# GRU steps 64 to 495 as loops on TensorE, with their side products in fp16 into one cleared PSUM bank

## The chip, the core and the metric

The kernel runs on one core of a Trainium2 chip, as one program. The metric is the device time in microseconds (us). TensorE has two instruction rows in the profile: PE (matmul) and PEld (weight load, beside the matmuls). DVE is VectorE, ACT is ScalarE, POOL is GpSimd, SP issues transfers.

## The reference, cut to what matters

The whole network is a top-k mask, attention, a GRU and a sampling layer, each added to x. The change touches the last two. x has four batches of 512 steps with 512 features.

```python
def cell(h, x):                       # 512 steps, one after the other
    gi = x @ W_ih + b_ih              # needs no h: "gates in"
    gh = h @ W_hh + b_hh
    i_r, i_z, i_n = jnp.split(gi, 3, axis=-1)
    h_r, h_z, h_n = jnp.split(gh, 3, axis=-1)
    r = jax.nn.sigmoid(i_r + h_r)
    z = jax.nn.sigmoid(i_z + h_z)
    n = jnp.tanh(i_n + r * h_n)
    h_new = (1.0 - z) * n + z * h
    return (h_new, h_new)
...
x = x + GRU(x)                        # this sum is x3 below
ix = (grid + 1.0) * 0.5 * (L - 1)     # then linear sampling along the features:
out = x + w0 * x[..., i0] + w1 * x[..., i1]
```

## The kernel before

The first third of the span (to 760 us) is mask and attention. Then come 512 GRU steps. Features lie on the 128 partitions, in four chunks; h is held as two halves A and B (two chunks each), each split into a high and a low fp16 part, so that the product with W_hh is made in fp16. One step on PE is 96 matmuls of 128 weights columns by 40 moving columns (L1924), in twelve units of eight named by GRU_UNITS: the half of h that is read, the half that is written, and the gate r, z or n. The units that read A come first (32 matmuls), then BA (24, which end the sums of half A), and the last unit is BBn.

What then happens to a half, taking B: the last matmul of BBn lets DVE sum h_n and r (a scan, L1477, `nlineB`); ACT makes the tanh (L930) and puts the next step's gates in into PSUM (L820, `putB`); DVE makes the new h (L1488) and its parts (L1499, `lowB`), which PE reads in the next step. ACT's program is in order: sigmoid A, give A, tanh A, sigmoid B, put A, give B, tanh B, put B, and then whatever else is due in that step.

Beside the recurrence stand side products, one chunk of a contraction per step behind PE's 96 matmuls: "gates" (x times W_ih for a coming stretch of 64 steps, L1832), "rows" and "late" (x3 times the sampling matrix, the output, L1859 and L1872), each an fp32 matmul of 256 moving columns. Four steps make a group. `side_plan` lists them: step 64 to 495 are full of them but for the steps 112 to 127, which have none. Steps 0 to 15 have three of 128 columns each. Groups alternate between two PSUM banks (`SIDE_BANK[number % 2]`); the first product of a group waits until the group two before it was taken (`side_taken`). ACT takes a group (L830 for gates, L841 for rows) behind its put B in the step in which its last product stands. The sampling matrix is made by ACT and POOL in steps 64 to about 106 (L861, L550). DVE adds the finished states to x (L1402).

The whole of PE's program is written out, instruction by instruction. DVE's is too, with alignments (L1453) in it.

## Time and profile before

| | us |
|---|---|
| median of three runs | 2282.22 |
| lowest and highest | 2280.85, 2285.1 |
| the profiled execution, its own time | 2288.73 |
| its span in the trace | 2286.8 |

The page says for every engine its busy time, then a chain of work followed back from the last instruction, then groups of instructions by line. PE has 95% of the span as busy time, the chain is PE at 81%, and more than half of the span is line L1924, the recurrence. A timeline lists instructions in order of time; "x8" means eight in a row, and the second column is from the start of the first to the end of the last. A bracket says how long the engine was idle before, and what ended that.

### The profile page before, as it was taken

What the parts mean: (1) busy time and instruction counts of PE and PEld (TensorE: products, weight loads), DVE (VectorE), ACT (ScalarE), POOL (GpSimd) and SP (SyncE); (2) the same over time, 40 slices, a digit from 0 to 9 for tenths busy, and PEclk for the clock granted to TensorE, in tenths of its full rate; (3) what the DMA queues carried; (4) which work ended last, traced back from release to release, by engine and by line L of the source; (5) the groups of instructions that cost most, each with busy time, mean ns of one, the idle gap of its engine ahead of it and who ended that gap; (6) DMA issues with size and microseconds to landing.
All of it is one profiled execution on the core that took longest, in us unless ns stands there. A gap on an engine that the chain in (4) does not pass through costs nothing.

```text
span 2286.8 us, 130730 instructions
## 1 busy us (share of the span) xinstructions
PE 2172.7 (95%) x56269; PEld 1831.7 (80%) x56269; DVE 1563.6 (68%) x6093; ACT 1207.0 (53%) x5574; POOL 504.3 (22%) x2271
## 2 busy tenths in 40 slices
PE   5768999999989999999999999999999999999998
PEld 3654655545545999999999999999999999999997
DVE  7987968869687466666666666666666667666665
ACT  6765947759467344566444444444444444444443
POOL 2002121021211122233222222222222222222222
PEclk8569999999999999999999999999999999999999
DMA  5000000010010000000000000000000000000000
GB/s 204 3 2 1 1 1 1 1 56 1 1 56 1 22 5 5 5 5 5 5 5 9 5 9 10 5 9 5 9 10 5 10 5 9 10 5 14 12 10 15
DMA packets 8715, 31.51 MB, mean 14 GB/s; under 512 B 1028, under 2 KB 1352, under 8 KB 7880
## 3 DMA queue, kind: packets, MB, share of 16 engines
q1 hardware_dynamic: 7712, 23.07, 2.7%
q8 instruction: 443, 7.26, 1.3%
q14 instruction: 136, 1.11, 0.2%
q10 hardware_dynamic: 424, 0.07, 0.0%
HBM read 18.94 MB, written 4.19 MB: 10 GB/s over the span
## 4 chain that ended last, share of the span: by engine, by line
PE 81%; DVE 12%; ACT 4%; issue 2%; DMA 1%; POOL 0%; SPq 0%; DVEq 0%; POOLq 0%; ACTq 0%
PE psum L1924 53%; PE psum L1832 9%; PE psum L1735 3%; PE psum L1656 3%; PE psum L1698 2%; PE psum L1753 2%; PE psum L1859 2%; PE psum L1719 2%; DVE region_cols L1087 2%; DVE region_cols L1103 2%; DVE top L1280 2%; ACT region_rows L751 1%; PE psum L1675 1%; DMA region_cols<-in_L_cond_W_emb_dram 1%; PE psum L1872 1%
## 5 line engine op out<-in xcount | busy, mean ns | idle before, releaser
L1924 PE MATMUL psum<-partsA,region_w_hh 128*128 128x40 f16 x24576 | 858.2, 179 | 7.2 <-issue 1.7
L1924 PE MATMUL psum<-partsB,region_w_hh 128*128 128x40 f16 x24576 | 858.2, 179 | 2.4 <-issue 1.9
L1924 PEld LDWEIGHTS psum<-partsA,region_w_hh 128*128 128x128 f16 x24576 | 761.7, 96 | 82.2 <-DVE partsA L1499 11.3
L1924 PEld LDWEIGHTS psum<-partsB,region_w_hh 128*128 128x128 f16 x24576 | 726.7, 95 | 5.4 <-issue 3.8
L564 POOL TENSOR_TENSOR region_w_b<-region_w_b 128x16 f32<-128x16 f32 x1022 | 242.6, 237 | 1135.5 <-DVE region_w_b L1488 1135.5
L1462 DVE TENSOR_REDUCE psum<-psum 128x8 f32<-128x32 f32 x1024 | 201.2, 197 | 292.5 <-PE psum L1924 291.3
L916 ACT ACTIVATE mixA<-psum 128x8 f32<-128x8 f32 x512 | 94.7, 185 | 549.7 <-DVE psum L1462 549.7
L930 ACT ACTIVATE region_w_b<-psum 128x8 f32<-128x8 f32 x1024 | 189.3, 185 | 151.2 <-DVE psum L1477 94.1
L1832 PE MATMUL psum<-region_cols,region_w_a 128*128 128x256 f32 (+1 forms) x864 | 252.7, 390 | 1.0 <-DVE region_cols L1269 0.9
L1488 DVE TENSOR_TENSOR_SCAN region_w_b<-giveB,region_w_b 128x40 f32<-128x40 f32 x512 | 123.6, 241 | 128.5 <-ACT region_w_b L930 128.5
L566 POOL COPY region_work<-region_w_b 128x8 f32<-128x8 f32 x1024 | 203.5, 199 | 2.2 <-DVE region_w_b L1488 2.2
L1469 DVE TENSOR_REDUCE psum<-psum 128x8 f32<-128x32 f32 x1024 | 191.1, 187 | 2.2 <-PE psum L1924 0.9
L751 ACT ACTIVATE region_rows<-psum,neg_top 128x512 f32<-128x512 f32 x256 | 173.9, 686 | 28.9 <-POOL neg_top L516 17.5
L1488 DVE TENSOR_TENSOR_SCAN region_w_b<-giveA,region_w_b 128x40 f32<-128x40 f32 x512 | 123.6, 241 | 75.1 <-ACT region_w_b L930 10.1
L1656 PE MATMUL psum<-region_w_a,region_work 128*128 128x512 f32 x384 | 173.7, 605 | 0.0
L1280 DVE TENSOR_REDUCE top<-psum 128x2 f32<-128x1024 f32 x128 | 156.1, 1221 | 22.9 <-PE psum L1719 22.7
L923 ACT ACTIVATE giveB<-psum 128x8 f32<-128x8 f32 x512 | 94.3, 184 | 102.1 <-DVE psum L1469 101.0
L1735 PEld LDWEIGHTS psum<-ident,region_rows 128*128 128x128 f32 x1024 | 119.0, 142 | 35.8 <-issue 19.0
L1477 DVE TENSOR_TENSOR_SCAN psum<-mixA,psum 128x32 f32<-128x32 f32 x512 | 117.0, 228 | 37.2 <-PE psum L1924 1.7
L1735 PE MATMUL psum<-ident,region_rows 128*128 128x128 f32 x1024 | 137.3, 276 | 5.1 <-ACT region_work L796 3.9
L1656 PEld LDWEIGHTS psum<-region_w_a,region_work 128*128 128x128 f32 x384 | 72.2, 193 | 82.7 <-issue 81.8
L1832 PEld LDWEIGHTS psum<-region_cols,region_w_a 128*128 128x128 f32 x864 | 123.4, 189 | 2.3 <-issue 2.1
(234 smaller groups left out, 2590.3 us busy)
## 6 DMA issues: line engine op xcount, KB each, us to landing
region_rows<-in_x_dram SPq DMA_DIRECT2D x4, 1024.0 KB, 11.1
region_w_a<-in_L_cond_W_qkv_dram SPq DMA_DIRECT2D x1, 3072.0 KB, 22.9
region_w_hh<-in_L_cond_W_hh_dram SPq DMA_DIRECT2D x4, 768.0 KB, 6.5
region_w_a<-in_L_cond_W_ih_dram SPq DMA_DIRECT2D x1, 3072.0 KB, 10.2
out_dram<-region_w_b SPq DMA_DIRECT2D x12, 256.0 KB, 3.1
region_cond<-in_cond_dram SPq DMA_DIRECT2D x2, 1024.0 KB, 7.9
region_cols<-in_L_cond_W_emb_dram SPq DMA_DIRECT2D x1, 2048.0 KB, 19.4
region_w_out<-in_L_cond_W_out_dram SPq DMA_DIRECT2D x1, 1024.0 KB, 21.5
```

Of the source, the lines that this page charges most:

```text
L564: e.tensor_tensor(k.line[half][:, :, :, 1:3], new.unsqueeze(3).broadcast_to([P, 2, B, 2]), k.signs.unsqueeze(1).unsqueeze(1).broadcast_to( ...
L566: e.tensor_copy(k.state[:, st + 1, 2 * half:2 * half + 2], new).then_inc(s[f"kept{h}"], 1)
L751: e.activation(k.probs[b][:, 2 * pair + i], k.bank(2 * pair + i, S), ACT.Exp, scale=logit_scale, bias=k.neg_top[:, col + i:col + i + 1], a ...
L930: e.activation(k.line[half][:, :, :, 0], k.nline[half][:, :, :, 3], ACT.Tanh, scale=unscale).then_inc(s[f"tanh{h}"], 1)
L1280: e.tensor_reduce(k.top[:, cols], k.psum[:, 2 * pair:2 * pair + 2], AX.X, ALU.max).then_inc(s["top"], 1)
L1462: e.tensor_reduce(k.rz[half][0], k.slots(R_BANK[half])[:, 0], AX.X, ALU.add).then_inc(s[f"rsum{h}"], 1)
L1469: e.tensor_reduce(k.rz[half][1], k.slots(Z_BANK[half])[:, 0], AX.X, ALU.add).then_inc(s[f"zsum{h}"], 1)
L1488: e.tensor_tensor_scan(k.spread[half].rearrange("p c b q -> p (c b q)")[:, 0::2], k.give[half][:].rearrange("p c b q -> p (c b q)"), k.lin ...
L1656: made = e.matmul(k.bank(bank, D), k.xnT[:, c, t * P:(t + 1) * P], k.w_qkv[:, c, i * D:(i + 1) * D], start=(c == 0), stop=(c == NC - 1))
L1735: made = e.transpose(k.bank(bank, NT, P)[:, kt], k.probs[b][:, slot, kt * P:(kt + 1) * P], k.ident[:])
L1832: made = e.matmul(k.bank(SIDE_BANK[number % 2], B * LENGTHS[q]), k.w_ih[:, c, block * P:(block + 1) * P], k.xT[:, c, :, STARTS[q]:STARTS[q ...
L1924: made = e.matmul(k.slots(bank)[:, :, ch, :, 0:2], k.w16[:, 2 * read + c, part, NC * "rzn".index(g) + 2 * half + ch], k.parts[read][:, c]. ...
```

## The change

In steps 64 to 495 PE's program is a loop around one step: six loops of 48 steps (gates), one of 16 steps without side products, sixteen of 8 steps (rows, late). One pass has 96 recurrence matmuls, four fp16 matmuls for the side products, four instructions that compute addresses from the loop's counter (L2205, L2207, L2209 and one at the loop's head, each with several register operations), an addition and a compare-and-branch. `addr_align` puts each loop's start on a multiple of 256 instructions.

The side products are fp16: each operand is split into a high and a low part, made by ACT (high) and DVE (low), and the one fp32 matmul becomes the four of high and low, 256 moving columns each. They all go to one bank, `SIDE_BANK[0]`, and accumulate there without a start flag on top of zeros that ACT writes (`act_clear`). The scales for the split come from maxima that DVE takes in steps 0 to 27, and from `in_scale` in steps 28 to 33, with PE waiting for DVE at the end of steps 28 and 29. W_ih is split in steps 35 to 59, x in pieces ahead of its stretch, x3 and the sampling matrix as they are made. The last 32 output rows and the 32 before them are made from such parts too (`pe_four_batches`).

```diff
@@ the plan
-    for q in range(2, CHUNKS):
-        s = STARTS[q]
-        for i in range(4):
-            if q + 1 < CHUNKS:
-                plan.append((s, [("gates", q + 1, j) for j in range(3 * i, 3 * i + 3)], 1))
...
+def loop_groups():
+    groups = []
+    for q in range(2, CHUNKS):
+        s = STARTS[q]
+        if q + 1 < CHUNKS:
+            groups += [("gates", s + NC * j, q + 1, j) for j in range(12)]
+            s += 12 * NC
+        if q > 2:
+            groups += [("rows", s + NC * i, 4 * (q - 3) + turn) for i, turn in enumerate(ROW_TURNS)]
+    for second in range(2):
+        groups += [("late", LATE_PRODUCTS + NC * (4 * second + i), 4 * second + turn) for i, turn in enumerate(ROW_TURNS)]
+    return groups
+LOOPED = STARTS[2]
+TAKE_STEPS = {group[1] + NC: n for n, group in enumerate(LOOP_GROUPS)}
+CLEARED = [group[1] + NC for group in LOOP_GROUPS]
@@ ACT
+def act_take_looped(e, k, n):
+    kind, _, *args = LOOP_GROUPS[n]
+    e.wait_ge(s["side_products"], NC * (n + 1))
+    if kind == "gates":
+        act_take_gates(e, k, *args, SIDE_BANK[0], None)
...
+def act_clear(e, k, n):
+    kind, _, *args = LOOP_GROUPS[n - 1] if n else ("gates", 0, 2, 10)
+    if kind == "gates":
+        e.wait_ge(s["gates_in"], 12 * args[0] + args[1] + 1)
+    else:
+        e.wait_ge(s["rows_out"], ROWS_TAKEN[n - 1])
+    e.activation(k.bank(SIDE_BANK[0], HALF_ROW), k.zero[:].broadcast_to([P, HALF_ROW]),
+                 ACT.Copy).then_inc(s["cleared"], CLEARED[n] - (CLEARED[n - 1] if n else 0))
@@ act_gru, behind put B of step st
+        if st in TAKE_STEPS:
+            act_take_looped(e, k, TAKE_STEPS[st])
+            if TAKE_STEPS[st] + 1 < len(LOOP_GROUPS):
+                act_clear(e, k, TAKE_STEPS[st] + 1)
+        if st == LOOPED - 4:
+            act_clear(e, k, 0)
@@ PE
+def pe_gate_loop(e, k, q):
+    first = STARTS[q - 1]
...
+    e.addr_align(PE_BLOCK, max_nops=4)
+    with e.Fori(0, 12 * NC) as turn:
+        weights = [w_parts[:, bass.ds(turn * (2 * P) + low * P, P)] for low in range(2)]
+        moving = [x_parts[:, bass.ds(turn % NC * HALF_ROW + low * NC * HALF_ROW, HALF_ROW)] for low in range(2)]
+        count = e.compute_val(turn + (first + 1))
+        pe_looped_step(e, k, count, weights, moving)
...
+        pe_looped_products(e, k, count, weights, moving)
+def pe_looped_step(e, k, count, weights, moving):
+    for u in GRU_UNITS:
+        if u == "AAr":
+            e.lower_ap(weights[0], for_matmul_weights=True)
+        if u == "BAr":
+            e.lower_ap(moving[0])
+        if u == "BBr":
+            e.lower_ap(weights[1], for_matmul_weights=True)
+        if u == "BBz":
+            e.lower_ap(moving[1])
+        pe_unit(e, k, u, count)
+def pe_looped_products(e, k, count, weights, moving):
+    to = k.bank(SIDE_BANK[0], HALF_ROW)
+    e.wait_ge(s["cleared"], count)
+    for stationary in weights:
+        for columns in moving:
+            made = e.matmul(to, stationary, columns, start=False, stop=True, skip_group_check=True)
+    made.then_inc(s["side_products"], 1)
...
+    if st == SCALE_AT:
+        e.wait_ge(s["in_scale"], 2)
+        e.wait_ge(s["gates_in"], 27)
+        e.transpose(k.bank(SIDE_BANK[0], P)[0:2], k.in_power[:], k.ident[:]).then_inc(s["in_turned"], 1)
@@ the last rows, and the 32 before them
+def pe_four_batches(e, k, bank, parts, part, c):
+    for low in range(2):
+        for sampled in range(2):
             for b in range(B):
+                made = e.matmul(k.bank(bank, HALF_ROW)[32 * b:32 * b + 32], parts[:, c, low, b],
+                                k.sampling[:, part, b, c, sampled],
```

ACT's program around a take, in the kernel before: region_w_b and region_scratch hold gates and lines, L820 is a put, L830 the take of a group of gates, and L916 begins the next step.

```order
L916 ACTIVATE mixB<-psum 128x8 [waits rsumB]
L820 ACTIVATE psum<-region_scratch 128x3x8 [waits nlineA]
L923 ACTIVATE giveB<-psum 128x8 [waits zsumB]
L930 ACTIVATE region_w_b<-psum 128x8 [waits nlineB]
L820 ACTIVATE psum<-region_scratch 128x3x8 [waits nlineB]
L830 ACTIVATE region_w_b<-psum,bias_in 128x256 [waits gates_in_sum]
L916 ACTIVATE mixA<-psum 128x8 [waits rsumA]
```

The same place in the changed kernel, where L855 is a put, L870 the take and L920 the clearing.

```order
L1061 ACTIVATE mixB<-psum 128x8 [waits rsumB]
L855 ACTIVATE psum<-region_scratch 128x3x8 [waits nlineA]
L1068 ACTIVATE giveB<-psum 128x8 [waits zsumB]
L1075 ACTIVATE region_w_b<-psum 128x8 [waits nlineB]
L855 ACTIVATE psum<-region_scratch 128x3x8 [waits nlineB]
L870 ACTIVATE region_w_b<-psum,bias_in,in_unscale 128x256 [waits side_products]
L920 ACTIVATE psum<-zero 128x256 [waits gates_in]
L1061 ACTIVATE mixA<-psum 128x8 [waits rsumA]
```

The take stood in the step with the group's last product; now take and clearing stand behind put B of the step after that, which is the first step of the next group.

PE's program in the kernel before, at the end of a step that begins a group of gates (L1832 is the fp32 side product) and the start of the next step.

```order
L1924 MATMUL psum<-partsA,region_w_hh 128x5x4x2 x7
L1924 MATMUL psum<-partsB,region_w_hh 128x5x4x2 x8
L1832 MATMUL psum<-region_cols,region_w_a 128x256 [waits gates_in]
L1924 MATMUL psum<-partsA,region_w_hh 128x5x4x2 [waits putA,lowA]
L1924 MATMUL psum<-partsA,region_w_hh 128x5x4x2 x7
```

The same place in the changed kernel: the end of the body of a gates loop (L2258 is the recurrence, L2219 the fp16 side product, ISA an address instruction).

```order
L2209 ISA
L2258 MATMUL psum<-partsB,region_w_hh 128x5x4x2 x8
L2258 MATMUL psum<-partsA,region_w_hh 128x5x4x2 x8
L2258 MATMUL psum<-partsB,region_w_hh 128x5x4x2 x8
L2219 MATMUL psum<-region_cond,region_rows 128x256 [waits cleared]
L2219 MATMUL psum<-region_cond,region_rows 128x256 x3
L2166 REGISTER_ALU
L2166 COMPARE_AND_BRANCH
```

One fp32 matmul that waited for the take of two groups before is now four fp16 matmuls behind a wait on `cleared`, and a branch follows. `cleared` must have reached the step's number plus one; clearing n lifts it to the end of group n, so the wait is new in a group's first step alone.

## Rows read from the trace of the kernel before

**Rows 1.** The page: the span, and the chain that ended last, by line.

```profile
span 2286.8 us, 130730 instructions
...
PE psum L1924 53%; PE psum L1832 9%; PE psum L1735 3%; PE psum L1656 3%; PE psum L1698 2%; PE psum L1753 2%; PE psum L1859 2%; PE psum L1719 2%; DVE region_cols L1087 2%; DVE region_cols L1103 2%; DVE top L1280 2%; ACT region_rows L751 1%; PE psum L1675 1%; DMA region_cols<-in_L_cond_W_emb_dram 1%; PE psum L1872 1%
```

**Rows 2.** Tile mixA, once a step, in three stretches: count, ns, first and last start.

```profile
L916 ACT ACTIVATE mixA<-psum x433: 183/185/187, 954.3 to 2229.5; 128x8 f32<-128x8 f32 x145
...
L916 ACT ACTIVATE mixA<-psum x17: 184/185/186, 1379.4 to 1426.2; 128x8 f32<-128x8 f32 x17
...
L916 ACT ACTIVATE mixA<-psum x9: 184/185/186, 1096.3 to 1118.8; 128x8 f32<-128x8 f32 x9
```

**Rows 3.** Timeline of a step's end with a take: start, us, engine, line, operation.

```profile
1247.60 0.35 PE L1924 MATMUL psum<-partsB,region_w_hh 128*128 128x40 f16 x8
...
1247.80 0.68 PE L1832 MATMUL psum<-region_cols,region_w_a 128*128 128x256 f32 x2
...
1247.99 0.23 DVE L1477 TENSOR_TENSOR_SCAN psum<-mixB,psum 128x32 f32<-128x32 f32 x1
...
1248.25 0.18 ACT L930 ACTIVATE region_w_b<-psum 128x8 f32<-128x8 f32 x1 [0.17 <-DVE psum L1477]
1248.31 0.96 PE L1924 MATMUL psum<-partsA,region_w_hh 128*128 128x40 f16 x32
1248.32 0.21 ACT L820 ACTIVATE psum<-region_w_b 128x24 f32<-128x24 f32 x1
...
1248.51 0.47 ACT L830 ACTIVATE region_scratch<-psum,bias_in 128x256 f32<-128x256 f32 x1
...
1249.51 0.20 DVE L1462 TENSOR_REDUCE psum<-psum 128x8 f32<-128x32 f32 x1 [0.58 <-PE psum L1924]
```

**Rows 4.** Lines L841 (take of rows, ACT) and L966 (a reduction, DVE).

```profile
L841 ACT ACTIVATE region_w_b<-psum x24: 383/383/385, 1189.4 to 2133.9; 128x256 f32<-128x256 f32 x24
...
L966 DVE TENSOR_REDUCE neg_max<-region_rows x4: 2272/2279/2286, 6.8 to 21.0; 128x4 f32<-128x2048 f32 x4
```

**Rows 5.** Timeline of the tail: the last additions and the last rows' products.

```profile
2277.14 1.44 DVE L1402 SCALAR_TENSOR_TENSOR region_cols<-region_work,h_unscale,region_cols 128x128 f32<-128x128 f32 x4 [0.35 <-POOL region_work L566]
...
2277.63 5.35 PE L1524 MATMUL psum<-region_rows,region_cols 128*32 128x256 f32 x64 [1.60 <-DVE region_cols L1402]
```

**Rows 6.** fp16 matmuls of 128 and 512 columns: one alone (ns), then sixteen and four.

```profile
L1675 PE MATMUL psum<-ident,region_cond x64: 217/219/229, 186.5 to 220.2; 128*128 128x128 f16 x64
...
L1719 PE MATMUL psum<-region_w_b,region_scratch x256: 377/379/634, 221.2 to 725.6; 128*128 128x512 f16 x128
...
210.69 1.06 PE L1675 MATMUL psum<-ident,region_cond 128*128 128x128 f16 x16
...
221.24 1.02 PE L1719 MATMUL psum<-region_w_b,region_scratch 128*128 128x512 f16 x4 [0.83 <-ACT region_w_b L736]
```

**Rows 7.** PE's idle times, and windows with the granted clock (the column before DMA's).

```profile
219.18 1.23 PE L1675 MATMUL psum<-ident,region_cond 128*128 128x128 f16 x16 [1.38 <-ACT region_scratch L736]
...
224.23 1.27 PE L1719 MATMUL psum<-region_w_b,region_scratch 128*128 128x512 f16 x2 [1.97 <-ACT region_rows L751]
...
218.00:222.00 4.00, 1.99 (x20) 1.30 (x20) 2.55 (x5) 2.05 (x3) 0.00 (x0) 1.00 0.00 0
222.00:226.00 4.00, 1.97 (x8) 1.06 (x7) 2.68 (x3) 2.60 (x8) 0.39 (x2) 0.68 0.00 0
...
2278.00:2282.00 4.00, 4.00 (x52) 2.15 (x48) 0.58 (x2) 0.38 (x1) 0.00 (x0) 0.57 0.01 1
```

**Rows 8.** Who waited for whom, 954 to 2229 us: PE's waits for issue.

```profile
PEld psum L1924 <- issue: 6.8, 26, 0.4
```

**Rows 9.** A branch (DVE), a register load (ACT), and the shortest transfer (KB, us).

```profile
L1453 DVEq COMPARE_BRANCH  x54: 41/41/47, 786.2 to 2253.3; - x54
...
L806 ACTq TENSOR_LOAD <-minus_gate_unscale x1: 277/277/277, 734.7 to 734.7; - x1
...
out_dram<-region_w_b SPq DMA_DIRECT2D x8, 32.0 KB, 1.6
```

More of the change, by code:

```diff
@@ L214, in __init__ @@
         self.banks = [self.psum[:, i] for i in range(8)]
[L215 removed]
+        kib = {"rows": 32, "cols": 32, "work": 32.25, "cond": 8, "w_a": 32, "w_b": 24,
                "w_hh": 24, "scratch": 16}
@@ new lines, in pe_row_loop @@
+def pe_row_loop(e, k, first, u, half):
+    s = k.sem
+    b = u % B
+    x3_parts = k.x3_parts[:, b:b + 2].rearrange("p b c l n -> p (b c l n)")
+    sampling = k.sampling[:, half, b:b + 2].rearrange("p b c l n -> p (b c l n)")
+    e.wait_ge(s["x3_lowered"], 2 * (u + 2))
+    e.wait_ge(s["hat_lowered"], 2 * NC * (b + 2))
+    e.addr_align(PE_BLOCK, max_nops=4)
+    with e.Fori(0, 2 * NC) as turn:
+        weights = [x3_parts[:, bass.ds(turn * (2 * P) + low * P, P)] for low in range(2)]
+        moving = [sampling[:, bass.ds(turn * (2 * HALF_ROW) + low * HALF_ROW, HALF_ROW)] for low in range(2)]
+        count = e.compute_val(turn + (first + 1))
+        pe_looped_step(e, k, count, weights, moving)
+        pe_looped_products(e, k, count, weights, moving)
@@ new lines, in pe_step, with pe_unit @@
+def pe_step(e, k, st):
+    s = k.sem
+    if st == 0:
+        e.wait_ge(s["gru_first"], 16)
+        e.wait_ge(s["w_kept"], NC)
+        e.wait_ge(s["w_low"], NC)
+    for u in GRU_UNITS:
+        pe_unit(e, k, u, st + 1)
+def pe_unit(e, k, u, count):
+    s = k.sem
+    read, h, g = "AB".index(u[0]), u[1], u[2]
+    half = "AB".index(h)
+    bank = {"r": R_BANK, "z": Z_BANK, "n": N_BANK}[g][half]
+    if u in ("AAr", "BAr"):
+        e.wait_ge(s[f"low{u[0]}"], count)
+    if u in ("AAr", "ABr"):
+        e.wait_ge(s[f"put{h}"], count)
+    for ch in range(2):
+        for c in range(2):
+            for part in range(2):
+                made = e.matmul(k.slots(bank)[:, :, ch, :, 0:2], k.w16[:, 2 * read + c, part, NC * "rzn".index(g) + 2 * half + ch],
+                                k.parts[read][:, c].unsqueeze(1).broadcast_to([P, COPIES, B, 2]),
+                                start=read == ch == c == part == 0, stop=(read == 1), skip_group_check=True)
+    if LAST_OF[g, h] == u:
+        made.then_inc(s[f"{g}_products{h}"], 1)
+    elif u == "ABn":
+        made.then_inc(s["readA"], 1)
```

469 lines of the change are left out of this document (319 added, 150 removed).

## The prediction, as it was put on record

> **What bounds the kernel now.** I read the page first, for what the span is made of, then how long one GRU step takes in each kind of stretch, then one step's end on the timeline, then the waits. The page gives a span of 2286.8 us, and over half of its last chain is L1924, the recurrence on PE [rows 1]. mixA is written once a step, so its starts are the step's clock [rows 2]. Sixteen undisturbed steps with side products go from 1379.4 to 1426.2: 46.8 / 16 = 2.925 us each. Eight steps without side products go from 1096.3 to 1118.8: 22.5 / 8 = 2.81 us. So the recurrence by itself (the matmuls of a half, then DVE, ACT, DVE, and PE again) needs 2.81 us, and a step with a side product is longer because PE is full: 96 matmuls and then the product. The 432 steps from 954.3 to 2229.5 take 1275.2 us. At those rates they would take 416 x 2.925 + 16 x 2.81 = 1261.8; the other 13.4 us are scattered hitches, of which PE's waits for issue are 6.8 [rows 8].
>
> The step's end [rows 3] tells what a side product costs and when ACT comes to its takes. The side product begins at 1247.80, just behind the last matmuls of the unit BBn, and the next step's first at 1248.31: 0.51 us. Meanwhile BBn's result goes through DVE (1247.99), the tanh (1248.25), put B (1248.32), and only then does ACT take a group (1248.51, for 0.47). That is 0.71 us behind the start of the side product. Before, nobody waited for this take: there are two banks, and PE needs this one a whole group later.
>
> **The change, part by part.**
>
> *The clearing.* Now there is one bank. ACT's take of group n and its clearing for group n+1 stand behind put B of the first step of group n+1, and PE's first product of group n+1, in that same step, waits for the clearing. Put B needs nlineB, which needs BBn, the last unit ahead of the wait: so the take can't have begun when PE comes to the wait, whatever the speeds are. PE then stands with everything behind it, the next step's matmuls included. The price, counted from where the side product began before: 0.71 to the take [rows 3]; 0.47 for the take [rows 3]; 0.07 until the clearing starts, since it waits for the take's own end (between 0.03, the DVE scan's end at 1248.22 to the tanh's start at 1248.25 [rows 3], and 0.35, DVE's wait behind POOL [rows 5]; nearer the first, as it is one semaphore); 0.38 for the clearing (the take of rows by ACT, also 256 columns, is 0.383 [rows 4]); and 0.13 until PE starts (the first of four additions ends at 2277.14 + 0.36 = 2277.50, PE starts at 2277.63 [rows 5]). Sum 1.76 us. Behind such a stop PE's sequencer has nothing in store, and the branch and the first address instruction come behind the products: I add 0.10, between 0 (all inside the products' 0.43 us) and 0.04 + 0.28, a branch on DVE and a register load on ACT [rows 9]. That makes 1.86 us per stop.
>
> There are 104 groups. The first is cleared in step 60, and the one at step 128 has 16 free steps ahead of it; the other 102 stop PE. 102 x 1.86 = 190 us. Step 496 waits for the last take in the same way, without a clearing: 0.71 + 0.47 + 0.13 = 1.3 us. Nothing gives this back: in the steps behind a stop PE is full as ever.
>
> *fp16 instead of fp32.* One alone lasts 219 ns at 128 columns and 379 at 512; sixteen take 1.06 and four 1.02 us [rows 6]. So they follow each other by (1.06 - 0.22) / 15 = 56 ns and (1.02 - 0.38) / 3 = 213 ns. On the line between, 256 columns are 108 ns, four are 0.43 us, 0.08 less than the 0.51 of before. The step goes to 2.845, still over the 2.81 of the recurrence, so all of it counts: 416 x 0.08 = 33 us gained. Bounds: 0 if a load of weights shows between them, 48 (0.115 a step) where the recurrence becomes the bound.
>
> *The loop.* If a pass through one aligned block needs no new instructions, PE's waits for issue go: 7 us gained, between 0 and all 13.4 of the hitches. Against that, a pass has four address instructions, an addition and a branch. In steps without a stop they lie beside 2.85 us of array work, and I cost them at nothing: the sequencer runs ahead. If that cover is gone, four at 0.04 to 0.28 and a branch of 0.04 [rows 9] are 0.2 to 1.2 us a step. On this the Trainium skill has two rules. Its page Advanced Engine Details and Errata (Control Flow Timing) puts a compare-and-branch at about 108 ns; an estimate by that page would add 432 x 0.108 = 47 us if none of it is covered. No row here has a branch on PE.
>
> *Preparation.* DVE takes 28 maxima of 512 columns in steps 0 to 27. 2048 columns take 2279 ns [rows 4], so one is 0.57 us, against DVE's idle 0.58 us in each step [rows 3]: at nothing, and 28 x 0.1 = 3 us if it does not fit. The splits (256 columns on DVE, 256 or 512 on ACT) are shorter than the idle time of those engines, too. In steps 28 and 29 PE waits for DVE's tail: DVE is free 1249.51 - 0.58 - 1248.31 = 0.62 us into the next step [rows 3], two small operations of 0.2 follow, so about 1.0 each: 2 us. The last rows get an ACT and a DVE operation between addition and product: 0.7 us (0 to 1.5).
>
> *The clock.* PE has not idled in the steps so far. The stops are 1.76 us of idle time, once in four steps. What did the granted clock do after such idle times? After 1.38 us (before 219.18) it stayed at 1.00 in 218 to 222; with 1.97 us before 224.23 it fell, 0.68 in 222 to 226; with 1.60 us before 2277.63 it fell too, 0.57 in 2278 to 2282 [rows 5, 7]. 1.76 lies among those that fell. 0.57 over 4 us means that it was at 1.2 instead of 2.4 GHz for 2 x 0.43 x 4 = 3.4 us. No row has a GRU step at 1.2 GHz. Bounds: the 40-column matmuls keep their pitch of 25 ns (rows 3: 32 in 0.96, eight in 0.35; 2.40 us for 96) and only the products double, 3.26 us a step, or all doubles, 5.7. I take an estimate between, 40 columns at 1.2 GHz = 33 ns: 3.2 + 0.86 = 4.05 us instead of 2.85, so 3.4 us at that clock lose 0.30 of themselves, 1.0 us (0.4 to 1.7). That two of three stops are followed by it is a guess from those three idle times: 68 x 1.0 = 68 us (0 to 102).
>
> *Sum.* + 190 + 1.3 - 33 - 7 + 2 + 0.7 + 68 = + 222 us. The profiled execution took 2288.7 and would take 2511; it was 6.5 over the median of its runs, so 2504 us is forecast. With the bounds of stop (1.6 to 2.1 us: -27, +24) and clock (-23, +34) this case spans 2454 to 2560.
>
> **The rivals.**
>
> *A. The stops without the clock.* The clock stays at 2.4 GHz through them, as after 1.38 us. 2504 - 68 = 2436 us. For it: PE would still be busy for 11.4 of the 13.2 us of four steps. Against: the 1.60 us idle time stood behind the same recurrence.
>
> *B. The loop shows in every step.* Sequencer work is not covered, say 0.15 us in each of 432 steps: + 65, 2569 us. For it: no row shows PE's sequencer doing such work. Against: right behind a side product 32 matmuls take 0.96 us [rows 3], the same pitch as eight in 0.35, (0.96 - 0.35) / 24 = 25 ns, so that the sequencer had them ready.
>
> *C. A taken branch has to fetch its block again.* The shortest transfer here is 1.6 us [rows 9]; behind 0.43 us of products that leaves 1.2 in each of 432 steps, + 518, about 3020 us. The Trainium skill has this as a rule, in Runtime: NRT & Kernel Launch (Instruction fetch mechanics): a taken branch whose target is not among the pages held stalls on a fetch by DMA. By that page the loops here, each inside one aligned block, would be held. No row shows a branch backward on any engine.
>
> *D. Faster.* PE does not stop at the wait, because the clearing is there in time. The price then is - 33 - 7 + 2 + 0.7 = - 37 and 2245 us. The point from which it decides is whether the clearing ends before PE's unit BBn does. That needs the clearing one step earlier than the order of ACT's program shows, so this is also the case in which I misread that order, or what the loop's count is compared with. For it: the new order is read from a program, and no trace shows it yet. Against: even the order of before has the take begin 0.71 us behind the side product [rows 3].
>
> **How the numbers follow.** Forecast 0.58, A 0.20, B 0.12, C 0.03, D 0.05, others 0.02. The predicted time is the forecast's. The range reaches down over most of A (its stop at 1.65 instead of 1.86 is 2415) and up to B's 2570: 2415 to 2570. A measurement of this kernel tells about 0.2%, 4.6 us, from no change. Faster is D alone, 0.05; within 0.2% would need a stop of under 0.45 us, less than the take alone, 0.01; slower 0.94.
>
> **What would show each step.** mixA's starts should come in a pattern of four: three of about 2.85 us and one of about 4.7. PE should be idle 1.7 to 1.9 us ahead of L2219 in a group's first step, released by ACT's L920, a hundred times, and nowhere in the steps 112 to 127. The pitch of L2219 should be 0.108 us. The granted clock of 954 us onward should be under 1.00, about 0.9 by my guess, with low spells behind the stops; 1.00 is A. Steps in the free loop should stay at 2.81; longer ones there, or over 2.87 in the second to fourth steps of a group at full clock, are B, and gaps of over a microsecond ahead of every step's first matmul are C. The prediction is wrong if PE passes the wait on `cleared` without idling, or if the time is under 2400.

## The result, and the profile after

The changed kernel is slower: 2480.4 us (median; 2478.9 to 2484.7) against 2283.7 for the kernel before on the same chip, a ratio of 1.086 (95% interval 1.084 to 1.089). 2504 was forecast, with a range of 2415 to 2570; the expected loss was 222 us, the measured one is 197. The profiled execution has a span of 2479.8 us, 193 more than [rows 1].

The page of the changed kernel: span, busy times, granted clock in tenths by slice, and the queue that brings instructions (packets, MB; 443 and 7.26 before).

```profile
span 2479.8 us, 135820 instructions
...
PE 2196.9 (89%) x57232; PEld 1865.5 (75%) x57232; DVE 1635.4 (66%) x6269; ACT 1296.7 (52%) x5763; POOL 525.8 (21%) x2255
...
PEclk8578999999999999999999999999999999999999
...
q8 instruction: 135, 2.21, 0.4%
```

PE is busy 24 us more than before, but the span has grown by 193: it is idle time that came in. The waits of the looped stretch, 954 to 2430 us (total, times, longest), name it.

```profile
PE psum L2219 <- ACT psum L920: 161.8, 102, 1.7
```

102 times PE stands ahead of the first side product (L2219) until ACT's clearing (L920) has ended: one stop for each group but two, as counted in the prediction. Now one step of the recurrence by mixA's starts. First fifteen steps' starts in the loop without side products, then a group's first step, then the three steps behind it.

```profile
L1061 ACT ACTIVATE mixA<-psum x15: 184/186/188, 1121.1 to 1160.3; 128x8 f32<-128x8 f32 x15
...
L1061 ACT ACTIVATE mixA<-psum x2: 187/188/188, 1205.9 to 1210.7; 128x8 f32<-128x8 f32 x2
...
L1061 ACT ACTIVATE mixA<-psum x4: 186/187/187, 1210.7 to 1219.2; 128x8 f32<-128x8 f32 x4
```

39.2 / 14 = 2.80 us in the free loop, as before (2.81, [rows 2]). 8.5 / 3 = 2.83 with four fp16 products (2.84 in the median of all such steps), where it was 2.925. And 4.8 in the step with the stop. This step on the timeline (start, length, then in brackets the idle time and what ended it; the first row is the unit BBn, whose last matmul the chain starts from):

```profile
1206.64 0.35 PE L2258 MATMUL psum<-partsB,region_w_hh 128*128 128x40 f16 x8
...
1207.37 0.21 ACT L855 ACTIVATE psum<-region_w_b 128x24 f32<-128x24 f32 x1
1207.51 0.56 ACT L870 ACTIVATE region_scratch<-psum,bias_in,in_unscale 128x256 f32<-128x256 f32 x1
...
1208.15 0.39 ACT L920 ACTIVATE psum<-zero 128x256 f32<-128x256 f32 x1
1208.60 0.61 PE L2219 MATMUL psum<-region_cond,region_rows 128*128 x4 [1.60 <-ACT psum L920]
1209.25 0.95 PE L2258 MATMUL psum<-partsA,region_w_hh 128*128 128x40 f16 x32
...
1211.65 0.60 PE L2219 MATMUL psum<-region_cond,region_rows 128*128 x4
1212.09 0.58 PE L2258 MATMUL psum<-partsA,region_w_hh 128*128 128x40 f16 x17
```

This is the chain of the prediction: put B, take (0.56 us), clearing (0.39), then PE. The last two rows are the next step's products, where nothing waits. There the recurrence follows 0.44 us behind the products' start; behind the stop it is 0.65. Over all stops that no low clock touches, the step is 1.93 us longer than 2.84 (median).

What the lower clock does is seen at another stop of the same kernel:

```profile
1221.93 1.01 PE L2219 MATMUL psum<-region_cond,region_rows 128*128 x4 [1.60 <-ACT psum L920]
1222.74 1.27 PE L2258 MATMUL psum<-partsA,region_w_hh 128*128 128x40 f16 x32
1223.84 1.23 PE L2258 MATMUL psum<-partsB,region_w_hh 128*128 128x40 f16 x32
...
1224.91 0.43 PE L2258 MATMUL psum<-partsA,region_w_hh 128*128 128x40 f16 x8
```

The window around it, where the third number from the right is the granted clock:

```profile
1221.00:1225.50 4.50, 3.57 (x87) 3.29 (x88) 1.54 (x8) 1.48 (x7) 0.55 (x2) 0.62 0.01 2
```

The idle time is the same 1.60 us, but the products now take 1.01 us instead of 0.61, and 32 matmuls of 40 columns 1.27 instead of 0.95. The granted clock is at 1.2 GHz here for 3.4 us (0.62 over 4.5 us). 36 of the 102 stops are followed by such a spell; a stop and the step behind it are then 0.85 us longer still.

The account of the 193 us, in spans:

| | forecast | in the trace |
|---|---|---|
| 102 stops | +190 | 102 x 1.93 = +197 |
| low clock behind stops | 68 x 1.0 = +68 | 36 x 0.85 = +31 |
| fp16 instead of fp32 | -33 | 416 x (2.925 - 2.843) = -34 |
| hitches inside the steps | -7 | -13, but +7 at the loops' ends |
| steps 0 to 63 | +2 | +4.6, of it 1.2 at the first loop's entry |
| steps 496 to 511, tail | +2.0 | +0.6, +1.0 |
| sum | +222 | +194 |

The first step of the recurrence also began 0.8 us earlier than before, which makes the sum 193.

### The profile page after: what moved, and what is told of

Its sections match the earlier page's. It is cut to its first block, busy times and chain, and to the rows that moved or that the text cites. A ratio compares the mean times of both kernels' runs of the same rounds, so it can differ in the third digit from the quotient of the medians.

```text
span 2479.8 us, 135820 instructions
## 1 busy us (share of the span) xinstructions
PE 2196.9 (89%) x57232; PEld 1865.5 (75%) x57232; DVE 1635.4 (66%) x6269; ACT 1296.7 (52%) x5763; POOL 525.8 (21%) x2255
## 4 chain that ended last, share of the span: by engine, by line
PE 76%; DVE 12%; ACT 8%; issue 3%; DMA 1%; POOL 0%; SPq 0%; ACTq 0%; POOLq 0%; DVEq 0%
PE psum L2258 50%; PE psum L2219 9%; PE psum L2005 3%; PE psum L1926 3%; PE psum L1968 2%; PE psum L2023 2%; PE psum L1989 2%; PE psum L2103 2%; ACT psum L920 2%; DVE region_cols L1248 2%; DVE region_cols L1232 2%; DVE top L1425 1%; DVE psum L1740 1%; ACT region_rows L786 1%; ACT region_w_b L1075 1%
## 5 line engine op out<-in xcount | busy, mean ns | idle before, releaser
L2258 PE MATMUL psum<-partsA,region_w_hh 128*128 128x40 f16 x24576 | 868.6, 181 | 12.5 <-issue 5.1
L2258 PE MATMUL psum<-partsB,region_w_hh 128*128 128x40 f16 x24576 | 864.3, 180 | 0.4 <-issue 0.4
L2258 PEld LDWEIGHTS psum<-partsA,region_w_hh 128*128 128x128 f16 x24576 | 768.8, 97 | 57.4 <-issue 27.3
L2258 PEld LDWEIGHTS psum<-partsB,region_w_hh 128*128 128x128 f16 x24576 | 735.4, 96 | 1.3 <-issue 0.7
L2219 PE MATMUL psum<-region_cond,region_rows 128*128 x1152 | 184.1, 284 | 112.4 <-ACT psum L920 112.4
L601 POOL COPY region_work<-region_w_b 128x8 f32<-128x8 f32 x1024 | 231.4, 226 | 2.2 <-DVE region_w_b L1751 2.2
L2219 PEld LDWEIGHTS psum<-region_cond,region_rows 128*128 x1152 | 93.0, 99 | 129.3 <-ACT psum L920 100.0
```

Source lines behind the costliest of these rows:

```text
L601: e.tensor_copy(k.state[:, st + 1, 2 * half:2 * half + 2], new).then_inc(s[f"kept{h}"], 1)
L2219: made = e.matmul(to, stationary, columns, start=False, stop=True, skip_group_check=True)
L2258: made = e.matmul(k.slots(bank)[:, :, ch, :, 0:2], k.w16[:, 2 * read + c, part, NC * "rzn".index(g) + 2 * half + ch], k.parts[read][:, c]. ...
```

## The experiments

Ratios are to the kernel before, measured beside it on the same chip. The chips differ a little (the kernel before took 2279 to 2286 us on them), so the ratios compare experiments better than the times do. Each trace is of one execution. All kernels but the two with a single fp32 matmul compute the whole result.

### Take and clearing one step earlier

```diff
-TAKE_STEPS = {group[1] + NC: n for n, group in enumerate(LOOP_GROUPS)}
+TAKE_STEPS = {group[1] + NC - 1: n for n, group in enumerate(LOOP_GROUPS)}
```

> Change: take and clearing of a group one step earlier, behind put B of the group's last step; all else as in the changed kernel. Theory (the stops at the wait on the clearing, and the low clock behind them, are the whole loss): the clearing then ends about 1.2 us into the next step, over a microsecond ahead of that step's products; no step of 4.76 us is left, steps are 2.84 throughout, the granted clock of steps 64 to 495 is 1.00, and the time is 2480 less 102 x 1.93 = 197 less 31 = about 2252 us, 31 below the kernel before. Rival 1 (the loops or the fp16 products cost something that the stops hide, and that then shows): stops gone but steps over 2.87 or longer loop ends, 2265 to 2290. Rival 2 (the stops are not caused by the place of the clearing): about 2480.

Measured: 2255.8 us, ratio 0.989 (0.987 to 0.991); 2252 was expected. The wait on the clearing is gone from the trace, and the granted clock is 1.00 from 954 us to the end of the last loop. One number moved the place of two ACT instructions by a step, and with it 225 us (223 by the ratios). So the stops and the clock behind them are the whole loss, and the rest of the change is a gain of about 26 us. A small loss was left: every eighth step of some stretches was 3.22 us and the next 2.68, 0.22 more than two of 2.84. ACT in such a step:

```profile
1012.92 0.56 ACT L870 ACTIVATE region_w_b<-psum,bias_in,in_unscale 128x256 f32<-128x256 f32 x1
...
1013.57 0.39 ACT L920 ACTIVATE psum<-zero 128x256 f32<-128x256 f32 x1
...
1013.89 0.71 ACT L962 ACTIVATE region_scratch<-region_scratch,ones 128x512 f32<-128x512 f32 x1
...
1014.50 0.16 ACT L1061 ACTIVATE mixA<-psum 128x8 f32<-128x8 f32 x1
...
1015.69 0.14 PEld L2258 LDWEIGHTS psum<-partsA,region_w_hh 128*128 128x128 f16 x3 [0.27 <-DVE partsA L1762]
```

Take, clearing and then a piece of the sampling matrix (L962) fill ACT until the next mixA is late, and at the step's end PE waits 0.27 us for partsA.

### ACT's other work out of the take's step

```diff
 # with the take one step earlier
-AWAY_STEPS = {HAT_AT + 8 * n + 2: n for n in range(HATS)}
-HAT_STEPS = {HAT_AT + 8 * n + 3: n for n in range(HATS)}
-DIAGONAL_STEPS = {HAT_AT + 8 * n + 4: n for n in range(HATS)}
+AWAY_STEPS = {HAT_AT + 8 * n + 1: n for n in range(HATS)}
+HAT_STEPS = {HAT_AT + 8 * n + 2: n for n in range(HATS)}
+DIAGONAL_STEPS = {HAT_AT + 8 * n + 3: n for n in range(HATS)}
...
-X3_STEPS = {P * (tile + 1) + 31 + 8 * b: B * tile + b for tile in range(NT - 1) for b in range(B)}
+X3_STEPS = {P * (tile + 1) + 30 + 8 * b: B * tile + b for tile in range(NT - 1) for b in range(B)}
```

> Change: take and clearing one step earlier, and ACT's work of 512 columns for the sampling matrix and for x3, which then stood in the same steps as a take (every second fourth step of many), one step earlier. Theory (in the steps of 3.22 us ACT's third operation, 0.71 us behind take and clearing, delays the next mixA, and with it PE, by about 0.22 net): 33 such pairs of steps gain 0.22 each, 2256 - 7 = about 2249 us, no step of 3.22 followed by 2.68 left. Rival (the 3.22 are from the loop's end, not from ACT): unchanged, about 2256.

Measured: ratio 0.985 (0.984 to 0.987), 2252.9 us where the kernel before took 2286.5. The pattern of 3.22 and 2.68 is gone, and the stretch of steps 64 to 495 went from 1238.4 to 1234.6 us, 3.8 and not the 7 expected. In the trace of the experiment before, only 20 of the long steps were followed by one of 2.68 (20 x 0.22 = 4.4); the other long ones, 3.1 to 3.2 us with a step of 2.84 behind them, are the loops' ends, and they stayed. So the rival held for those. This is the fastest version by its median, 34 us ahead of the kernel before. The two intervals nearly touch, and the two profiled executions as a whole differ by 0.7 us, so what the trace shows is that the pattern went and what it was worth in these steps; that the whole time is shorter for it is likely, not shown.

### The take alone one step earlier

The take stands in the group's last step, the clearing stays in the next group's first step.

```diff
-TAKE_STEPS = {group[1] + NC: n for n, group in enumerate(LOOP_GROUPS)}
+TAKE_STEPS = {group[1] + NC - 1: n for n, group in enumerate(LOOP_GROUPS)}
...
         if st in TAKE_STEPS:
             act_take_looped(e, k, TAKE_STEPS[st])
-            if TAKE_STEPS[st] + 1 < len(LOOP_GROUPS):
-                act_clear(e, k, TAKE_STEPS[st] + 1)
+        if st - 1 in TAKE_STEPS and TAKE_STEPS[st - 1] + 1 < len(LOOP_GROUPS):
+            act_clear(e, k, TAKE_STEPS[st - 1] + 1)
```

> Change: the take alone one step earlier; the clearing stays behind put B of the group's first step. The stop is then without the take: 1.93 - 0.47 - 0.07 = 1.39 us, 102 x 0.54 = 55 us saved. Theory on the clock (whether it falls depends on how long PE stands): 1.39 us stayed at full clock before, so few or no low spells, another 31 us saved, about 2394 us, and a granted clock of 1.00. Rival (it falls by something else than the length of the stop, at 36 of 102 as now): about 2425 us and a clock near 0.96. If the stop isn't the sum of the ACT chain: it stays 1.9, about 2480.

Measured: 2384.4 us, ratio 1.046 (1.044 to 1.048). The stop is 1.30 us instead of 1.93, 0.63 less (a take of gates is 0.56 and not the 0.47 I still used, and the 0.08 behind it), and not one of 102 stops is followed by a low clock. By the chain alone 102 x 0.63 = 64, with the clock's 31 it is 95; measured 96, or 93 by the ratios.

### Longer stops

```diff
 def act_clear(e, k, n):
...
+    e.activation(k.bank(SIDE_BANK[0], HALF_ROW), k.zero[:].broadcast_to([P, HALF_ROW]), ACT.Copy).then_inc(s["padded"], 1)
+    e.wait_ge(s["padded"], n + 1)
     e.activation(k.bank(SIDE_BANK[0], HALF_ROW), k.zero[:].broadcast_to([P, HALF_ROW]),
                  ACT.Copy).then_inc(s["cleared"], CLEARED[n] - (CLEARED[n - 1] if n else 0))
```

> Change: ACT writes the zeros twice, the second waiting for the first, and only the second counts; computed result unchanged. Theory: each stop is longer by a clearing and a wait, 0.38 + 0.07 = 0.45 us, 2.38 in all: 102 x 0.45 = 46 us. If the clock depends on the length of the stop: nearly all of 102 stops are followed by a low spell instead of 36, 66 x 0.86 = 57 us more: about 2583 us, clock about 0.87 in steps 64 to 495. If it does not depend on it: the same 36, about 2526 us and 0.96. If the stop isn't the sum of ACT's chain: about 2480.

Measured: 2530.3 us, ratio 1.111 (1.108 to 1.114), near the 2526 of a clock that does not depend on the length, and far from 2583. Next the same extra clearing with the take moved out:

> Change: the take one step earlier, the clearing behind put B of the group's first step as before but made twice, the second waiting for the first; computed result unchanged. Each stop is then 1.32 + 0.45 = 1.77 us, and PE's idle time ahead of the products 0.94 + 0.45 = 1.39 us, between the 0.94 that was followed by a low clock 0 times of 102 and the 1.60 that was 36 times. Theory (the longer the idle time the more often a low clock; 1.38 us stayed at full clock in the kernel before): 0 to 20 of 102, 2384 + 46 + 0 to 17 = 2430 to 2447 us. Rival (a threshold-like jump below 1.4): 36 or more, over 2460.

Measured: 2481.0 us, ratio 1.088 (1.085 to 1.090); the rival's time holds. And two extra clearings in the changed kernel:

> Change: ACT writes the zeros three times, each waiting for the one before, and only the last counts; computed result unchanged. PE's idle time ahead of the products is then 1.60 + 0.90 = 2.5 us, 102 times: 2480 + 102 x 0.9 = 2572 by the chain alone. Theory (low spells rise with the idle time: 0 of 102 at 0.94, 36 at 1.60, 45 at 2.01): 50 to 70 of 102 followed by a low clock, 2572 + 20 = about 2590 us. Rival (every stop of over two microseconds is followed by it): 102 of 102, about 2630. Rival 2 (no further rise): about 45, 2580.

Measured: 2619 us (2609 and 2630), ratio 1.148 (1.142 to 1.154). This lies between the theory (50 to 70 low spells, 2590) and the first rival (102, 2630); the second rival (no further rise) is out. Below are the waits for the clearing from 954 to 2430 us: first of the kernel with the take alone moved, then of one extra clearing in the changed kernel, of one extra with the take moved, and of two extra. The looped stretch of the second and the fourth ends later than 2430, so their 100 and 95 are not all of their 102 stops. Then come the windows 1180 to 2400 us of the same four (the first one's span ends at 2384):

```profile
PE psum L2219 <- ACT psum L920: 96.7, 102, 1.0
```

```profile
PE psum L2221 <- ACT psum L922: 200.3, 100, 2.1
```

```profile
PE psum L2221 <- ACT psum L922: 145.6, 102, 1.5
```

```profile
PE psum L2223 <- ACT psum L924: 230.0, 95, 2.5
```

```profile
1180.00:2400.00 1220.00, 1104.97 (x37696) 1048.30 (x37696) 739.96 (x3895) 563.02 (x3244) 301.34 (x1500) 1.00 0.01 4
```

```profile
1180.00:2400.00 1220.00, 1043.13 (x34504) 990.48 (x34500) 688.08 (x3588) 565.15 (x3084) 278.37 (x1384) 0.95 0.01 3
```

```profile
1180.00:2400.00 1220.00, 1087.73 (x35711) 1031.78 (x35708) 714.06 (x3709) 576.99 (x3184) 285.97 (x1426) 0.94 0.01 4
```

```profile
1180.00:2400.00 1220.00, 1018.07 (x32845) 966.15 (x32842) 660.10 (x3416) 573.25 (x3020) 263.42 (x1316) 0.92 0.01 3
```

All five kernels side by side, counted over the whole looped stretch of one trace each (stop: median over those without a low clock; time: median of all executions):

| PE's idle time at a stop, us | stop, us | of 102 followed by 1.2 GHz | us |
|---|---|---|---|
| 0.94 | 1.30 | 0 | 2384 |
| 1.42 | 1.78 | 51 | 2481 |
| 1.60 (the changed kernel) | 1.93 | 36 | 2480 |
| 2.01 | 2.34 | 45 | 2530 |
| 2.43 | 2.76 | 76 | 2619 |

Two things follow. The chain is additive: a clearing with its wait is 0.48 (1.30 to 1.78), 0.41 (1.93 to 2.34) and 0.42 us (to 2.76). And the clock is no simple function of the stop's length. At 0.94 us it never fell; at 1.42 it fell more often than at 1.60, which is why the kernel whose stops are shorter by 0.15 us is not faster (51 spells at 0.92 us there, 47 us, against 36 at 0.85, 31 us). The counts change from one execution to the next: with two extra clearings the mean clock was 0.922 in the profiled execution and 0.903 in the other, which took 21 us more. That 51 is more than 36 stands, since the changed kernel had 0.944 to 0.948 in its four executions and the kernel at 1.42 us 0.935 and 0.936; the order of 45 and 51 is not told. Within the changed kernel, the stops with and without a low spell had the same median of 1.60 us, and stops of 1.50 and of 1.69 are in both kinds. The stop right behind one with a spell had one as well 3 times of 36 in the changed kernel and 9 of 51 at 1.42 us, but 30 of 45 at 2.01. What picks the one from the other is open: no run here varies it by itself.

### The loops written out

```diff
-    e.addr_align(PE_BLOCK, max_nops=4)
-    with e.Fori(0, 12 * NC) as turn:
-        weights = [w_parts[:, bass.ds(turn * (2 * P) + low * P, P)] for low in range(2)]
...
+    for turn in range(12 * NC):
+        weights = [w_parts[:, turn * (2 * P) + low * P:turn * (2 * P) + low * P + P] for low in range(2)]
...
```

The other two kinds of loop likewise. In a first form `addr_align` stayed:

> Change: the three kinds of loop on PE written out, 432 steps one after the other, no address instruction, no branch; order, products and waits as in the changed kernel. Theory (the loop costs nothing inside a step, 0.3 to 0.4 us at each of 22 loop ends and 1.2 at the first entry, and saves 7 to 13 us of waits for issue): about 2480, between 2470 and 2490, with the same 102 stops of 1.9 us, perhaps 1.8 since nothing has to be computed behind the stop. Rival (address instructions and branch show in every step or behind every stop, 0.1 us and more): 2480 less 102 x 0.1 to 432 x 0.1 = 2437 to 2470.

Measured: 2531.8 us, ratio 1.110 (1.106 to 1.113): 50 us slower, which neither theory had. The loss stands where the loops began, as here at the start of what was the loop of steps 456 to 463:

```profile
2315.27 0.60 PE L2211 MATMUL psum<-region_w_a,region_rows 128*128 128x256 f16 x4
2317.75 0.90 PE L2250 MATMUL psum<-partsA,region_w_hh 128*128 128x40 f16 x30 [1.88 <-issue]
```

```profile
L2184 PEldq COMPARE_BRANCH  x16: 1018/2633/3043, 1328.6 to 2437.0; - x16
```

```profile
L2184 PEldq COMPARE_BRANCH  x16: 304/307/334, 1327.4 to 2391.9; - x16
```

Each of the long ones has a 16 KB packet of the instruction queue landing in or just before it and ends 1.34 to 1.50 us behind that landing; beside the short ones there is none. The branch back to the start of a gates loop is another record:

```profile
L2166 PEldq COMPARE_BRANCH  x288: 76/211/257, 958.8 to 2200.2; - x144
```

In the changed kernel PE waits 0.24 us at the same place as above:

```profile
2255.00 0.60 PE L2219 MATMUL psum<-region_w_a,region_rows 128*128 x4
2255.84 0.95 PE L2258 MATMUL psum<-partsA,region_w_hh 128*128 128x40 f16 x32 [0.24 <-issue]
```

Without any alignment:

> Change: the changed kernel with its stops, loops on PE written out, without any alignment. Theory (alignment jumps were the written-out kernel's loss; behind a stop the loop costs 0.17 us more than written-out code, 1.93 against 1.76, since addresses and branch have to be worked through with nothing ahead): 2480 - 102 x 0.17 - 8 - 1 + 10 = about 2464 us. Rival (straight code behind stops is late in itself): about 2530.

Measured: ratio 1.084 (1.082 to 1.085), 2476.4 us; the changed kernel's 1.086 (1.084 to 1.089) is not told from it. Without the alignments the written-out kernel is 2.6% faster than with them. Here a stop is 1.76 us and not 1.93, and the recurrence follows the products 0.45 us behind their start:

```profile
1188.80 0.61 PE L2208 MATMUL psum<-region_cond,region_rows 128*128 128x256 f16 x4 [1.59 <-ACT psum L920]
1189.25 0.96 PE L2247 MATMUL psum<-partsA,region_w_hh 128*128 128x40 f16 x32
```

So with a loop each stop costs 0.17 us more. That branch and first address then come when nothing is in store is the likely reason; no run takes them apart. The 17 us did not show in the time: this run had 43 low spells behind its stops and not 36 (10 us), and waits for issue in its steps. That the loops made no difference beside the stops did not mean that they are worth nothing, as the same pair without stops showed:

> Change: take and clearing one step earlier, and the three kinds of loop on PE written out, without any alignment. Theory (the 50 us that the written-out kernel with stops lost were jumps of the alignments to instructions not yet there, and without stops the loops are worth no more than the waits for issue, 7 to 13 us, less the loops' ends, 22 x 0.35 = 8): 2250 to 2265 us, steps of 2.84, no wait for issue of over 1.5 us. Rival (code written out is slow by itself, with fp16 products the instructions don't come fast enough): over 2270, waits for issue all along.

Measured: 2307.5 us, ratio 1.009 (1.007 to 1.011): the rival. The loops are worth 2.0% or 46 us once the stops are gone. The waits of the written-out kernel (954 to 2195 us; its looped stretch lasts to 2257 and the profiled execution was 10 us over the median), then three of its places on the timeline:

```profile
PEld psum L2247 <- issue: 47.5, 143, 0.9
PE psum L2247 <- issue: 30.3, 104, 0.8
...
1523.53 0.88 PE L2247 MATMUL psum<-partsB,region_w_hh 128*128 128x40 f16 x29 [0.82 <-issue]
...
1527.54 0.19 PE L2247 MATMUL psum<-partsB,region_w_hh 128*128 128x40 f16 x1 [0.31 <-issue]
...
1535.51 0.53 PE L2247 MATMUL psum<-partsA,region_w_hh 128*128 128x40 f16 x15 [0.27 <-issue]
```

The waits are mostly 4 or 8 us apart (74 of 112 distances), somewhere among the 40-column matmuls. They are waits for instructions: the instruction queue brings 339 packets of 16 KB in this stretch, one in about 3.8 us, and 109 of PE's 113 waits for issue end 1.30 to 1.65 us behind the landing of one. With the loops it is 23 packets, as many as there are loops. Yet the kernel before is written out too, has 333 such packets, and had 6.8 us of waits [rows 8]. What differs are the products. The next run takes the four out and puts one fp32 matmul in (identity with itself, so that the gates and rows of steps 64 on are missing from its result):

```diff
-    for stationary in weights:
-        for columns in moving:
-            made = e.matmul(to, stationary, columns, start=False, stop=True, skip_group_check=True)
+    made = e.matmul(to, k.ident[:], k.ident[:].rearrange("p (o n) -> p o n", o=1).broadcast_to([P, 2, P]), start=False, stop=True, skip_group_check=True)
```

> Change: take and clearing one step earlier, written out without alignment, and in place of the four fp16 products of a step a single fp32 matmul of 256 columns, of the identity matrix with itself, so that the gates and rows of steps 64 on are left out and the result is another one. It has 3 matmuls and 3 weight loads fewer a step than the written-out kernel of 2307 us, and each step's array work is 0.08 us longer. Theory (written-out code with four short products is late because TensorE is short of instructions, about 0.3 us at every 4 us; one long product is the time in which it catches up, as in the kernel before): steps of 2.925, waits for issue of 5 to 15 us in all, 2256 + 34 + 5 = about 2295 us, no slower than the written-out fp16 one. Rival (written-out code pays those waits whatever the products): 2307 + 34 = about 2340.

Measured: 2292.9 us, ratio 1.005 (1.004 to 1.007), as the theory had it, with, from 954 to 2195 us,

```profile
PEld psum L2245 <- issue: 8.1, 35, 0.7
PE psum L2245 <- issue: 2.4, 9, 0.6
```

The same edit in the kernel with its loops:

> Change: take and clearing one step earlier, loops kept, and in place of a step's four fp16 products the single fp32 matmul of 256 columns (identity with itself), so that the gates and rows of steps 64 on are left out and the result is another one. The fourth corner beside loop with fp16 (2256), written out with fp16 (2307) and written out with fp32 (2293). Theory (the two parts of the change need each other: fp16 alone makes written-out code wait for instructions, a loop alone has little to save): steps of 2.925, 416 x 0.08 = 33 more than loop with fp16 and none of written-out fp32's extra waits: 2256 + 33 = about 2289 us, 4 below written-out fp32. Rival (the loop is worth 50 us by itself, whatever the products): 2293 - 50 = about 2243. Rival 2 (a loop with one long product loses its addresses' cover): over 2300.

Measured: 2282.9 us, ratio 1.000 (0.999 to 1.001), nearest to the theory's 2289. With it the square is full, all four with take and clearing one step earlier:

| ratio to the kernel before | written out | loops | worth of the loops |
|---|---|---|---|
| one fp32 matmul | 1.005 | 1.000 | 0.5%, 12 us |
| four fp16 products | 1.009 | 0.989 | 2.0%, 46 us |

The two parts of the change need each other. fp16 products in loops gain 1.1%, 26 us; in written-out code they gain nothing and probably lose 0.3% (the two intervals, 1.004 to 1.007 and 1.007 to 1.011, touch), since PE then waits for instructions. What runs short is the fetch, by the landings above. The fp32 matmul is 0.5 us of array work from one instruction, during which the instructions catch up; that reading agrees with the square, but no run varies the length alone. The fp32 matmul here has two equal operands, and its step was 2.92 us, as the 2.925 of before.

### The addresses in one place

```diff
 # with the take one step earlier
 def pe_looped_step(e, k, count, weights, moving):
     for u in GRU_UNITS:
-        if u == "AAr":
-            e.lower_ap(weights[0], for_matmul_weights=True)
...
 def pe_looped_products(e, k, count, weights, moving):
     to = k.bank(SIDE_BANK[0], HALF_ROW)
+    for low in range(2):
+        e.lower_ap(weights[low], for_matmul_weights=True)
+        e.lower_ap(moving[low])
     e.wait_ge(s["cleared"], count)
```

> Change: take and clearing one step earlier (no stops), and the four address computations one behind the other just ahead of the products instead of spread over the units. Theory (the sequencer's register work lies beside the array's work as long as it runs ahead, and that is all four at once too): steps 2.84 us as with them spread, about 2256 us. Rival B of the prediction in this form (register work is covered only where it is spread): each step is longer by what isn't covered, 0.05 to 0.5 us, 416 x 0.05 to 0.5 = 21 to 208 us more, 2277 to 2460.

Measured: 2312.5 us, ratio 1.011 (1.010 to 1.013), 52 us more than with the four spread out (2.3%). The step is 2.96 instead of 2.84 (median of its mixA periods). Its waits (954 to 2195 us) and one step's end:

```profile
PEld psum L2253 <- issue: 52.7, 213, 1.6
...
1503.39 0.60 PE L2214 MATMUL psum<-region_w_a,region_rows 128*128 x4
1503.92 0.75 PE L2253 MATMUL psum<-partsA,region_w_hh 128*128 128x40 f16 x24
```

0.53 us from the products to the next step's first matmul, where it was 0.44. PE's weight loads also waited 49.3 us for DVE's partsA, against 13.3 with the addresses spread; whether that follows from the first is not shown. What PE has in store covers one address computation at a time, but not four. So rival B's mechanism is real; spreading is what keeps the changed kernel out of it.

## Why the prediction was right, point by point

- **The stop.** Right in place, cause and number: 102, by the order of ACT's program. Term by term, at the stop shown above: from where the products would have begun, 0.20 behind BBn's start at 1206.64, to the take 0.67 (forecast 0.71 from [rows 3]); the take 0.56 for gates and 0.47 for rows (forecast 0.47, from a take that had no scale operand; with one, both kinds are 0.09 longer); 0.08 to the clearing (0.07); the clearing 0.39 (0.38, [rows 4]); 0.06 until PE starts (0.13, from [rows 5]); the restart 0.65 - 0.44 = 0.21 (0.10). In sum 1.97, which is what this step is longer (4.81 by mixA's starts, less 2.84), and 1.93 in the median of all stops, against 1.86. The take and the restart were too small, by 0.09 and 0.11, the wait of PE and the way to the take too large, by 0.07 and 0.04: part of the agreement is that these cancel. Moving the take out took 0.63 off, and each added clearing put 0.41 to 0.48 on, so the terms are causes and not a fit.
- **fp16.** Four products take 0.44 us (forecast 0.43) and the step is 2.843 (2.845). The interpolation between 128 and 512 columns [rows 6] held.
- **The loop.** "If a pass through one aligned block needs no new instructions" held: the instruction queue carried 135 packets instead of 443, and no wait of a transfer's length stands behind a branch, so rival C is out; for loops of one held page that is also what the Trainium skill's page Runtime: NRT & Kernel Launch (Instruction fetch mechanics) had given. In the steps nothing shows of the address instructions and the branch, as forecast; the Trainium skill's page Advanced Engine Details and Errata (Control Flow Timing), by which an uncovered compare-and-branch would, as an estimate, add 47 us, has no trace in the 2.84 us of a step. The branch is covered and not short: its own record is 211 ns in the median (shown with the written-out loops), longer than the 108 ns of that page of the Trainium skill. What I had not priced: 0.35 us at the end of each of 22 loops (7 us) and 1.2 us at the first loop's entry. With the hitches all gone (13.4) the net gain is 5 us and not 7. But the worth of the loop was sized against the wrong neighbour. Against written-out fp16 code it is 46 us, because that code waits for its instruction packets and the kernel before hardly did.
- **The clock.** The mechanism was right and the size twice too large: 36 low spells for the 68 guessed, 0.85 us each for 1.0. The bound of -23 us had no working, and the truth was 37 below. The three idle times of [rows 7] did not allow a share. Neither did they allow the line that I drew between 1.38 (stayed) and 1.60 (fell): 1.42 fell 51 times of 102. The 40-column matmuls at 1.2 GHz went at (1.27 - 0.43) / 24 = 35 ns, 33 was estimated. This term alone would have put the forecast 37 us too high; the stops (+7) and the steps ahead of the loops (+3) took some of it back. The time came out 24 us under the forecast. The truth lies between the forecast and rival A (2436).
- **Preparation and ends.** Steps 27, 28 and 29 were 0.2, 0.9 and 1.4 us longer (2 forecast; PE's weight loads waited 1.1 and 1.3 us for DVE's `in_power` and `in_diagonal`), the stop in step 496 was 1.28 (1.3), of which 1.1 shows in that step's length, the tail 1.0 (0.7).
- **Rival D** named the point from which the sign turns: "the clearing one step earlier than the order of ACT's program shows", for 2245 us. With exactly that done it was 2256, ratio 0.989, and 2253 with ACT's work moved out of the way. That is a gain of 26 us and not 37, as the loops' ends (7), their entry (1.2) and ACT's full steps (4) were not in the rival's sum.

## What to carry to other kernels

Where one engine must empty and clear a buffer before another may go on, look at the order of the first one's program and not at its idle time: here ACT was idle half of the span, and two instructions of 0.95 us in the wrong step cost 225 us, in the step before they cost nothing. Price each part of a change beside the other parts, too: short products without the loop gain nothing, the loop without them has little to save, and a large stop hides what either is worth. And register work on TensorE's sequencer is free only in small portions: four address computations cost nothing spread over a step and 0.12 us a step in one place.

## What the runs showed of the hardware that was not expected

- A granted clock of 1.2 GHz followed idle times of 1.4 us in 51 of 102 cases though TensorE was busy for over 11 us between them, never those of 0.94 us, and its share did not rise evenly with the length (51, 36, 45, 76 of 102 at 1.42, 1.60, 2.01, 2.43 us, one execution each). Each spell cost 0.85 to 0.97 us of the recurrence, whose 40-column matmuls went from 25 to 35 ns.
- Straight code of 100 matmuls with their weight loads in 2.84 us waited for instructions, 113 times in 432 steps, some 0.3 us each, and 109 of the waits ended 1.30 to 1.65 us behind the landing of a 16 KB instruction packet; the same in a loop of one aligned block did not wait inside its steps, and 97 of them in 2.925 us, the last one long, hardly did.
- A jump forward in straight code to an aligned address lasted 1.0 to 3.3 us by its own record, with a packet landing each time; the jump from one loop to the next, with none, lasted 0.31 and cost about 0.35.
- A backward branch on TensorE lasted 0.21 us in the median by its own record, and none of it showed in the steps of 2.84 us.
- Behind a stop, a loop's body took 0.2 us longer to restart than written-out code.
- A per-partition scale from memory made ACT's take of 256 columns 0.09 us longer (0.47 to 0.56, 0.38 to 0.47).
